# Value products in pairs of slots, three probability buffers, and two loads moved to SyncE's queue, in an attention and mixture kernel

## What is computed

```
x = x + attention(layernorm(x), ctx, ctx)        # 16 heads of 16; 1601 keys; scores*tau + delta per key; softmax
x = x + experts(layernorm(x))                    # top 1 of 8, all eight computed, gated sum
x = x + tanh(cat(window_attention(ctx, layernorm(x)), layernorm(x)) @ W_c.T)
x = x + slots(layernorm(x))                      # router to 64 slots, top 8, a small recurrence on the slots
```

## Time and profile before

| | |
|---|---|
| median of 3 runs | 1020.42 us (1019.92 to 1021.2) |
| profiled execution | 1020.56 us, its span 1018.9 us |
| TensorE busy | 957.2 us, 94% |
| VectorE busy | 741.1 us, 73% |
| ScalarE busy | 562.0 us, 55% |
| GpSimd busy | 65.8 us, 6% |

### The profile page before, as it was taken

How to read it: one execution, slowest core, us unless ns; L and a number is a source line. 1 busy time by engine, 2 the same in 40 slices (tenths; PEclk the granted TensorE clock), 3 DMA queues, 4 the chain that set the end, 5 groups by cost and what they waited for, 6 DMA issues and landing times.

```text
span 1018.9 us, 13739 instructions
## 1 busy us (share of the span) xinstructions
PE 957.2 (94%) x4794; PEld 385.9 (38%) x4794; DVE 741.1 (73%) x1704; ACT 562.0 (55%) x1063; POOL 65.8 (6%) x94
## 2 busy tenths in 40 slices
...
GB/s 208 193 77 101 144 17 16 1 17 23 15 17 1 1 16 1 17 1 58 1 17 1 17 1 16 1 13 46 16 1 1 1 1 43 1 135 1 0 104 82
DMA packets 34586, 36.19 MB, mean 36 GB/s; under 512 B 6971, under 2 KB 31592, under 8 KB 34258
## 3 DMA queue, kind: packets, MB, share of 16 engines
...
...
## 4 chain that ended last, share of the span: by engine, by line
PE 74%; issue 10%; DVE 7%; ACT 5%; DMA 1%; DVEq 1%; POOL 1%; ACTq 0%; SPq 0%; POOLq 0%
PE ps_o L1210 18%; PE ps_m L1127 16%; PE ps_e L1416 14%; PE ps_m L1314 8%; DVE mx L1721 4%; PE ps_m L1416 3%; ACT probs L909 3%; PE ps_m L1273 2%; PE ps_e L1083 2%; PE ps_m L1263 1%; PE ps_m L1360 1%; PE ps_m L1363 1%; DMA probs<-in_ctxT 1%; PE ps_m L1219 1%; PE ps_m L1230 1%
## 5 line engine op out<-in xcount | busy, mean ns | idle before, releaser
L1721 DVE TENSOR_REDUCE mx<-ps_m 128x1 f32<-128x401 f32 x1024 | 530.3, 567 | 136.5 <-PE ps_m L1127 131.7
L909 ACT ACTIVATE probs<-ps_e 128x512 f32<-128x512 f32 (+1 forms) x685 | 392.0, 600 | 280.0 <-PE ps_e L1416 278.5
L1127 PE MATMUL ps_m<-k_stack,q_stack 99*128 99x401 bf16 x1024 | 303.6, 338 | 9.7 <-DVE mx L1721 7.0
L1416 PE MATMUL ps_e<-q_stack,k_stack 101*128 101x512 bf16 (+1 forms) x685 | 261.0, 386 | 7.0 <-ACT probs L909 4.6
L1210 PE MATMUL ps_o<-probs,v_heads 128*32 128x512 f32 (+1 forms) x1664 | 223.9, 610 | 0.3 <-ACT probs L909 0.3
L1127 PEld LDWEIGHTS ps_m<-k_stack,q_stack 99*128 99x128 bf16 x1024 | 100.7, 98 | 158.1 <-DVE mx L1721 102.3
L1416 PEld LDWEIGHTS ps_e<-q_stack,k_stack 101*128 101x128 bf16 (+1 forms) x685 | 67.2, 99 | 223.0 <-ACT probs L909 137.7
L909 ACT ACTIVATE probs<-ps_m 128x512 f32<-128x512 f32 (+1 forms) x147 | 88.2, 600 | 23.8 <-PE ps_m L1416 23.8
L1314 PE MATMUL ps_m<-expert_w,xnT 128*128 128x512 f32 x192 | 99.1, 597 | 0.7 <-DVE xb L1859 0.7
L1416 PE MATMUL ps_m<-q_stack,k_stack 101*128 101x512 bf16 (+1 forms) x147 | 56.5, 385 | 6.6 <-ACT probs L909 3.6
L1210 PEld LDWEIGHTS ps_o<-probs,v_heads 128*32 128x32 f32 (+1 forms) x1664 | 32.9, 108 | 68.0 <-issue 35.1
...
## 6 DMA issues: line engine op xcount, KB each, us to landing
...
xres<-in_x SPq DMA_DIRECT2D x4, 512.0 KB, 3.8
x<-xres SPq DMA_DIRECT2D x4, 512.0 KB, 3.0
...
probs<-in_ctxT SPq DMA_DIRECT2D x3, 512.0 KB, 9.4
...
```

Source lines behind the costliest of these rows:

```text
L909: act.activation(probs[0:n, k % 2, h, :], score_bank(c, k, h)[0:n, :], ACT.Exp).then_inc(s["exp_done"], 1)
L1127: pe.matmul(ring_bank((n1, u))[:, 0:SPLIT], qst[0:MAX_ROW, g, h, P * t:P * t + P], kst[0:MAX_ROW, HG * g + h, QUARTER_START[q]:QUARTER_STA ...
L1416: pe.matmul(score_bank(c, k, h)[0:n, :], kst[0:ROWS, HG * g + h, P * st:P * st + n], qst[0:ROWS, g, h, :], start=True, stop=True).then_inc ...
L1721: dve.tensor_reduce(mx[:, q, col:col + 1], ring_bank((n1, u))[:, 0:SPLIT], AX.X, ALU.max)\
```

## The change

- `values_behind(c, k)`: in a group's slots 2, 4, ... 12 the value products of the two slots before are issued together at the slot's end; slots 1, 3, ... 11 issue none; slot 0 issues that of slot 12 of the group before. There are 96 such pairs and 16 single products.
- `probs` has three buffers, by the running slot number modulo 3, and the exponentials of a slot wait for the value product three slots back.
- Chunk 0 takes its maxima by `BY_PAIRS` (4 in slots 0 and 1, then 6 and 4 by turns, 6 in the even ones); `BY_LOAD` is a new table for the other chunks, with the same sum.
- The delta rows of groups 1 and 2 and the ones rows are issued by SyncE: the first before the load of `xb`, the second behind it and ahead of the stores of q.
- To make room for the third buffer, `keep`, `gauss`, `delta_a` and `delta_b` lie in tiles that are used later (`hT`, `wc`). Their instructions are the same.

```
-EVEN = [NG * UNITS * (k + 1) // SLOTS - NG * UNITS * k // SLOTS for k in range(SLOTS)]
-BY_LOAD = [5, 6, 4, 7, 7, 1, 1, 6, 7, 7, 1, 7, 7,
+BY_PAIRS = [4, 4] + [6, 4] * 5 + [6]
+BY_LOAD = [5, 4, 7, 6, 7, 1, 2, 4, 7, 4, 5, 6, 7,
...
-    per_slot = BY_LOAD if c else EVEN
+    per_slot = BY_LOAD if c else BY_PAIRS * NG
...
+def values_behind(c, k):
+
+    st = k % ST
+    if st == 0:
+        return [k - 1] if k or c else []
+    return [k - 2, k - 1] if st % 2 == 0 else []
...
-        probs_raw = sb("probs", [P, 2 * HG * CT])
-        probs = probs_raw[:].rearrange("p (b h t) -> p b h t", b=2, h=HG)
+        probs_raw = sb("probs", [P, 3 * HG * CT])
+        probs = probs_raw[:].rearrange("p (b h t) -> p b h t", b=3, h=HG)
...
             move_k(sp, 1, rows, k_loaded[1])
+            sp.wait_ge(s["delta_stored"], 16)
+            sp.dma_start(kst[DELTA_ROW:DELTA_ROW + 3, HG:3 * HG, :], d_parts[:, 0:S].unsqueeze(1).broadcast_to((3, 2 * HG, S)))\
+              .then_inc(delta_loaded[1], 16)
             sp.wait_ge(s["xnT_ready"], 2)
             sp.dma_start(xb[:], x_dram[:, 3 * TT:4 * TT, :]).then_inc(x_start[1], 16)
+            sp.wait_ge(s["consts_set"], 1)
+            sp.dma_start(kst[MAX_ROW:MAX_ROW + 2, 0:3 * HG, :], ones_sb[0:2, 0:S].unsqueeze(1).broadcast_to((2, 3 * HG, S)))\
+              .then_inc(s["ld_k"], 16)
...
-                if step == ("L", 2):
-                    load_delta(1)
-                    pool.dma_start(kst[MAX_ROW:MAX_ROW + 2, 0:3 * HG, :],
-                                   ones_sb[0:2, 0:S].unsqueeze(1).broadcast_to((2, 3 * HG, S))).then_inc(s["ld_k"], 16)
...
-                act.activation(probs[0:n, k % 2, h, :], score_bank(c, k, h)[0:n, :], ACT.Exp).then_inc(s["exp_done"], 1)
+                act.activation(probs[0:n, (SLOTS * c + k) % 3, h, :], score_bank(c, k, h)[0:n, :], ACT.Exp).then_inc(s["exp_done"], 1)
...
-                    need(act, s["pv_done"], SLOTS * c + k - 1)
+                    need(act, s["pv_done"], SLOTS * c + k - 2)
...
-                    if k or c:
-                        pv(c, k - 1)
+                    for j in values_behind(c, k):
+                        pv(c, j)
```

More of the change, by code:

```diff
@@ L311, in build @@
         iota_w = scratch[:, W:2 * W]
-        keep = sb("keep", [P, W])
-        gauss = sb("gauss", [P, W])
+        keep, gauss = (hT[:, W * i:W * i + W] for i in range(2))
         neg_mask = sb("neg_mask", [P, W])
@@ L340, in build @@
         rtau = sb("rtau", [P, 2])
-        delta_a, delta_b = sb("delta", [ST, P]), sb("delta_rest", [ST, P])
+        delta_a, delta_b = (wc[0:ST, 0, P * i:P * i + P] for i in range(2))
         delta3 = sb("delta_parts", [ST, 3, P], BF16)
@@ L757, in low_of @@
                 pool.tensor_tensor(part(b, 2), rest[:, b % 2, 0:n], part(b, 1), ALU.subtract).then_inc(s["blk_parts"], 1)
-            def load_delta(i):
-                pool.wait_ge(s["delta_stored"], 16)
-                groups = (1, 2)[i]
-                pool.dma_start(kst[DELTA_ROW:DELTA_ROW + 3, HG * i:HG * (i + groups), :],
-                               d_parts[:, 0:S].unsqueeze(1).broadcast_to((3, HG * groups, S))).then_inc(delta_loaded[i], 16)
             scale_shift(0)
-            load_delta(0)
+            pool.wait_ge(s["delta_stored"], 16)
+            pool.dma_start(kst[DELTA_ROW:DELTA_ROW + 3, 0:HG, :], d_parts[:, 0:S].unsqueeze(1).broadcast_to((3, HG, S)))\
+                .then_inc(delta_loaded[0], 16)
             pool.wait_ge(s["window_start"], 1)
@@ L1689, in masks @@
                 if i == 1:
-                    dve.tensor_scalar(keep[:], iota_w[:], win_f[:, 5:6], None, ALU.is_ge)
-                    dve.tensor_scalar(gauss[:], iota_w[:], win_f[:, 6:7], None, ALU.is_le)
+                    dve.tensor_scalar(keep, iota_w[:], win_f[:, 5:6], None, ALU.is_ge)
+                    dve.tensor_scalar(gauss, iota_w[:], win_f[:, 6:7], None, ALU.is_le)
                     dve.drain()
@@ L1695, in masks @@
                     dve.drain()
-                    dve.tensor_tensor(keep[:], keep[:], gauss[:], ALU.mult)
+                    dve.tensor_tensor(keep, keep, gauss, ALU.mult)
                     dve.drain()
-                    dve.tensor_scalar(neg_mask[:], keep[:], -1.0, BIG, ALU.add, ALU.mult)
+                    dve.tensor_scalar(neg_mask[:], keep, -1.0, BIG, ALU.add, ALU.mult)
                     dve.tensor_tensor(iota_w[:], iota_w[:], iota_w[:], ALU.mult).then_inc(s["masks_ready"], 1)
```

22 lines of the change are left out of this document (11 added, 11 removed), and 6 rows, old and new, of the table BY_LOAD.

## The result

The changed kernel takes 1032.73 us (median of 4 runs, 1029.88 to 1034.19) against 1020.17 us in the same comparison: ratio 1.0122, 95% interval 1.0094 to 1.015. The forecast was 1009 us, and 0.79 stood on faster. It was wrong in sign: +12.6 us instead of -11.5. The prediction took a change under 0.2% for none, from three runs that lay within 0.13%.

The account below looks back on a forecast made before the run. The prediction took VectorE and three ring banks to bound chunk 0, a mixture the other chunks. Its terms, 6 - 11 - 6.5 = -11.5 on the profiled 1020.56, gave 1009 us, range 999 to 1019.

Parts of the forecast that it names:

- term 3: Chunks 1 to 3: pairs with the new table shorten them by 11 us, bounds 0 and -20.
- term 4: The start: without GpSimd's wait for its loads it is 6.5 us shorter, bounds -8 and +2.5.
- term 2: Chunk 0: products in one piece leave VectorE waiting behind three ring banks; +6 us, bounds +3 and +8.
- Bound: Chunk 0 is set by VectorE and the three ring banks, the other chunks by a mixture, slot by slot.
- Term 1: Product pairs on TensorE: each saves 0.2 us, 19 us for 96 pairs if TensorE were all.
- The rival of the held-up `xb`: The start: moved loads delay `xb`, so it gives nothing or loses 2.5 us; 1015 to 1018 us, chance 0.15.
- The two samples: Chunk 1, group 0: slots 7 and 8 forecast at 6.74 us, slots 5 and 6 at 5.4.
- the rule: Each slot or pair takes the longest of three sums of work, for TensorE, VectorE and ScalarE.
- Starved VectorE in chunks 1 to 3: Products in one piece starve VectorE there too, +13 us in 48 stretches; 1028 us in all, chance 0.13.
- TensorE sets it after all: TensorE alone sets the time: -19 us in all chunks, -6.5 at the start; 995 us, chance 0.12.

Follow-up runs that it names:

- e5: The changed kernel with each maxima reduction of VectorE over 200 of 401 columns; 987.34 us.
- e6: e2 with each maxima reduction of VectorE over 200 of 401 columns, single products in all chunks; 986.74 us.
- e1: The kernel before with only the loads of the delta and ones rows moved to SyncE; 1012.65 us, ratio 0.9937.
- e11: e4 with the pairs of chunks 1 to 3 moved to the ends of the odd slots and slot 0; 1025.82 us, ratio 1.0059.
- e4: The changed kernel with single products and the even split of maxima in chunk 0 alone; 1025.93 us, ratio 1.0069.
- e2: e1 with the new `BY_LOAD` table in chunks 1 to 3, three buffers and single products; 1013.75 us, ratio 0.995.
- e13: e12 with one pair per chunk put back, the products of slots 4 and 5 of group 2; 1005.44 us, ratio 0.9877.
- e3: e1 with pairs in chunks 1 to 3 and the old table, single products in chunk 0; 1024.02 us, ratio 1.0053.
- e12: Kernel before with moved loads, `xb` first, mixed table, pairs only in groups 1 and 2 of chunks 1 to 3, except slots 4, 5 of group 2; 1001.53 us.

## Why the prediction was wrong

**The range.** Its upper end doesn't follow from its own terms: term 3 at half, term 4 near zero and term 2 at 8 give 1020.56 - 5.5 + 8 = 1023, not 1019. The result lies outside either.

**Bound.** Right for chunk 0, and right that "98% busy" isn't a kernel that TensorE alone sets. e5 and e6 show VectorE as the limit of chunk 0.

**Term 1, right in size.** 0.24 to 0.25 us at pairs where TensorE sets the pace (slots 1 and 2 or 9 and 10 of group 1), against 0.2; over the six pairs of group 1 it is 0.13 on average. The two products start to start 1.86, against 1.87. The Trainium skill, TensorEngine Tiling (Array Packing), Key Properties, says that a change of the tiling mode drains TensorE, and not one of the tile alone. The trace agrees: in the pair at 97.43 the four passes start 0.43 to 0.45 us apart, across the border of the two products as within one, and the score product, in another mode, starts 0.55 behind the last.

**Term 2, right.** +6.6 against +6; pairs at 6.26 against 6.27; 1.34 of idle against 1.4.

**Term 4, right in sum, wrong in what was left.** -6.4 against -6.5. The drain was the wait, as e1 shows. But the delta rows ahead of `xb` cost more than I took: `xb` lands 8.6 to 11.9 us after its issue with them ahead (eleven executions) and 7.2 to 8.1 with them behind (three). The start then lost between nothing (e11) and some 3 us (e4: a wait of 1.99 us, and the clock at 0.50 behind it). The rival of the held-up `xb` was thus at work, but small beside the 9 us of the drain. The Trainium skill, DMA: Bandwidth & Descriptors, Why a DMA increments its semaphore by 16 and not by 1, has the three delta rows on three engines; the later landing agrees with that, but would with any sharing too.

**Term 3, the step that failed.** "Over all: 209.9, 210.0 and 195.3 us, against 212.2, 212.9 and 198.8", made -11, and was +11.9 (659.7 - 647.8). The two samples themselves held nearly: slots 5 and 6 of group 0 take 5.27 us (5.4 forecast), slots 7 and 8 take 7.05 (6.74). What the rule left out were three things:

- The table. It was made by the sums of work per stretch: +4.6 us apart from the clock in the profiled executions (e2 against e1; 3 to 5 over all), where the rule had it as part of a gain. It stands at slots 5 and 6 of group 2, which cost 1.90 us in each chunk, 5.7 in all, against 1.3 gained elsewhere: one unit in the slot where ScalarE holds TensorE up, seven in the next.
- Waits within a stretch. The rule takes the longest of three sums, as if TensorE could always do something else while it waits. In single slots the value product was that something. "Of the 23 us that the rule leaves open now I let a tenth go" had these waits shrink; e13 shows one of them growing by 0.86 us as its block moves away. If TensorE had set the pace everywhere, the 72 pairs of chunks 1 to 3 would have saved 17 us (72 x 0.24). Apart from the clock they cost 1.4 to 1.8 us in the profiled executions (e2 to e4, e1 to e3), and 2 to 6 by the medians of all. VectorE has 4 to 5 us of that distance of some 20 (e5, e6); the rest is such waits and slots whose time TensorE doesn't set, and wasn't measured apart.
- The clock. Pairs raised the time at 0.50 in chunks 1 to 3 from 13.7 to 30.7 us with the old table, from 3.4 to 23.9 with the new, and from 3.4 to 27.3 with half reductions: 8.5 to 12 us at half a us each. Over all executions of e1 to e4 it is 16 and 21 us more, 6 to 10 us of time, more than half of what the pairs cost there. I used the clock in Term 4 and not in Term 3, although show 0.99 and 0.98 in chunks 2 and 3.

**The rivals.** *Starved VectorE in chunks 1 to 3* gave 1028 us, nearest to the result, but for a cause that has 4.7 us there, where it had 13. *TensorE sets it after all* holds in part of groups 1 and 2, which is what e12 uses. That the longer waits make the clock fall was no rival of mine.

**Open.** Why the clock falls at some of these places in one chunk and not in another (e13: chunk 2, not 1 and 3) isn't settled. What is shown is that the falls in groups 2 and 3 come during or within 4.5 us behind waits of TensorE that sum to 0.9 to 2.6 us, and that those at slots 9 and 10 of group 0 have no wait above 0.13 us ahead of them. The waits alone don't decide it: e2 waits 1.47 and 0.55 us at slots 5 and 6 of group 2, more than the 0.77 and 1.07 of the changed kernel, and its clock stays at 1.00 there in all three chunks. That pairs bring more time at 0.50 is shown by the runs; by what property of them isn't.
